# Moving SiLU, one-hot weighting and the causal mask of a transformer tower to GpSimd

## The reference, cut to what matters

```
h = tok(x)
h = h + L0_attn(layernorm(h))
h = h + L0_ffn(layernorm(h))       # routed part: silu(x w1) * (x w3), weighted, summed over tokens
h = h + L1_attn(layernorm(h))      # scores att, causal; polymax below
h = h + L1_ffn(layernorm(h))       # rms norm, ternary up, gelu, rms norm, ternary down

def polymax(x):                    # masked scores are -inf and give 0
    lin  = where((x >= -100) & (x <= 0), -0.01 * x + 1, 0)
    poly = where(x > 0, x ** 2 + 1, 0)
    return (poly + lin) / 1000
```

## Time and profile before

| | before |
|---|---|
| median of 3 runs | 842.32 us |
| the profiled execution, its own time | 843.61 us |
| its span, first to last instruction | 841.5 us |
| mean granted TensorE clock | 0.933 |
| TensorE busy in products | 735.3 us (87%) |
| VectorE busy | 647.9 us (77%) |
| ScalarE busy | 409.8 us (49%) |
| GpSimd busy | 77.9 us (9%), 68 instructions |

### The profile page before, as it was taken

One profiled execution on the slowest core, in us unless ns is written; L12 is line 12 of the kernel. 1 busy time (PEld: TensorE's weight loads), 2 busy tenths in 40 slices (PEclk: granted clock), 3 DMA queues, 4 the chain that ended last, 5 costly groups with the idle time before them and its releaser, 6 DMA issues.

```text
span 841.5 us, 24887 instructions
## 1 busy us (share of the span) xinstructions
PE 735.3 (87%) x10567; PEld 514.5 (61%) x10567; DVE 647.9 (77%) x1447; ACT 409.8 (49%) x609; POOL 77.9 (9%) x68
## 2 busy tenths in 40 slices
PE   5879999999999999975795788999998999997857
PEld 3456666667676757654384556566765756565634
DVE  7667878888878888677586778988888998587653
ACT  4536454555546473542223282845547382644513
POOL 1101111110202020100000001000101001010000
PEclk9869999999999999975875999999999999999969
DMA  9024202020202000200000000000000000000000
GB/s 323 12 95 156 76 0 75 0 75 0 75 0 75 0 0 6 97 2 1 1 2 1 2 2 26 3 26 3 0 25 0 25 2 26 2 26 2 20 9 26
DMA packets 7371, 27.22 MB, mean 32 GB/s; under 512 B 2320, under 2 KB 3216, under 8 KB 5776
## 3 DMA queue, kind: packets, MB, share of 16 engines
q1 hardware_dynamic: 7312, 26.35, 8.4%
HBM read 22.15 MB, written 4.19 MB: 31 GB/s over the span
## 4 chain that ended last, share of the span: by engine, by line
PE 60%; DVE 22%; issue 9%; ACT 8%; DMA 0%; POOL 0%; DVEq 0%; POOLq 0%; SPq 0%; ACTq 0%
PE PS L372 10%; PE PS L321 6%; PE PS L741 6%; PE PS L383 5%; PE PS L476 4%; PE PS L706 4%; PE PS L362 4%; PE PS L465 3%; PE PS L418 3%; PE PS L433 3%; DVE mx L1290 3%; DVE Pm L1296 2%; ACT w_s L1015 2%; PE PS L451 2%; PE PS L683 2%
## 5 line engine op out<-in xcount | busy, mean ns | idle before, releaser
L890 ACT ACTIVATE PT<-PS 128x512 f32<-128x512 f32 x64 | 36.8, 596 | 78.4 <-PE PS L465 78.4
L362 PE MATMUL PS<-ident_s,xn 128*128 128x128 f32 x256 | 48.2, 304 | 25.5 <-DVE xn L1211 22.3
L719 PE MATMUL PS<-xT,wqkv_h 128*128 128x512 f16 x256 | 63.7, 394 | 6.0 <-ACT w_s L1015 4.5
L321 PE MATMUL PS<-tokW_h,w_s 128*128 128x256 f16 x504 | 58.5, 273 | 0.0
L883 ACT ACTIVATE Pm<-Pm 128x1024 f32<-128x1024 f32 x32 | 33.5, 1056 | 51.3 <-DVE Pm L1296 51.3
L362 PEld LDWEIGHTS PS<-ident_s,xn 128*128 128x128 f32 x256 | 31.0, 149 | 38.1 <-DVE xn L1211 21.0
L321 PEld LDWEIGHTS PS<-tokW_h,w_s 128*128 128x128 f16 x504 | 48.7, 98 | 5.8
L741 PE MATMUL PS<-tokW_h,work 128*128 128x256 f16 x448 | 51.4, 273 | 0.5 <-issue 0.5
L1290 DVE TENSOR_REDUCE mx<-PS 128x16 f32<-128x1024 f32 x32 | 39.0, 1220 | 16.3 <-PE PS L433 16.2
L372 PE MATMUL PS<-xT,wat_h 128*128 128x512 f16 x192 | 46.2, 400 | 4.5 <-DVE xT L1592 4.5
L719 PEld LDWEIGHTS PS<-xT,wqkv_h 128*128 128x128 f16 x256 | 22.7, 100 | 44.0 <-ACT w_s L1015 17.9
(11 more groups left out here) (245 smaller groups left out, 1636.8 us busy)
## 6 DMA issues: line engine op xcount, KB each, us to landing
work<-in_x SPq DMA_DIRECT2D x7, 1536.0 KB, 6.9
out<-H SPq DMA_DIRECT2D x8, 512.0 KB, 2.6
w_s<-in_w SPq DMA_DIRECT2D x3, 1024.0 KB, 7.0
work<-in_x SPq DMA_DIRECT2D x3, 512.0 KB, 5.9
wup_s<-in_wup SPq DMA_DIRECT2D x1, 1024.0 KB, 4.8
wdn_s<-in_wdn SPq DMA_DIRECT2D x1, 1024.0 KB, 8.3
w_s<-in_tokW SPq DMA_DIRECT2D x3, 256.0 KB, 4.1
wup_s<-in_wqkv SPq DMA_DIRECT2D x1, 768.0 KB, 7.5
```

What stands on the lines that cost most here:

```text
L321: m = pe.matmul(dst, halves_[xi][:, k, rows], w[:, wi, k, cols], start=(n == 0), stop=(n == 3 * chunks - 1))
L362: m = pe.transpose(PS[:, bank, t * P:(t + 1) * P], xn[:, t, c * P:(c + 1) * P], ident_s[:, :])
L719: m = pe.matmul(PS[:, UP_BANKS[f % 3], :], wup_h[:, c, f * P:(f + 1) * P], part[:, c, :], start=(k == 0), stop=(k == 2 * C - 1))
```

## The change

1. The mask products on TensorE (`identb`, `cmaskb`) are gone, and the score products start fresh. GpSimd subtracts the mask (-1e30) from the linear part in SBUF instead, in place, one instruction of 128x1024 f32 per tile (`mask_later`, 32 in all), and `poly` waits for it (`masked`). Masked positions then hold about 1e30, and (lin <= 1) makes them 0.
2. Both linear parts of tiles 0 and 1 are taken by VectorE (`v_lin`), none of them by ScalarE. For tiles 2 and 3 ScalarE takes the linear part before the square.
3. `silus` leaves VectorE. On GpSimd it is two instructions per half, a product and a sum (`silu`), four per routed slot. `weighted_hots` goes to GpSimd too, at the end of the slot before.
4. `stats3` of a slot's input is done a slot ahead, behind `v_x4T`, and `norm3` is then the first work of a slot.
5. `norm4` has two small steps in the place of four. `poly` of tiles 0 and 1 stands behind all eight `g_parts`, not with four of them between.

```
@@ B2_scores @@
                 elif t == 2:
-                    pe.wait_ge(lin_ok, 3 * g + 1)
-                    pe.wait_ge(linv_ok, g + 1)
+                    pe.wait_ge(linv_ok, 2 * g + 2)
                 hb = (t % 2) * 256
-                for i in range(4):
-                    pe.matmul(PS[:, i, hb:hb + 256], identb[:, :], cmaskb[:, :, :], start=True, stop=False,
-                              skip_group_check=True)
...
-                                          start=False, stop=True, tile_position=(32 * i, 0), skip_group_check=True)
+                                          start=True, stop=True, tile_position=(32 * i, 0), skip_group_check=True)
@@ scalar: a_B3, slot_B @@
                         relus(g + 1, 1)
-                        lins(g + 1, 0)
...
                 for t in (2, 3):
                     relus(g, t)
+                    lins(g, t)
                     quads(g, t)
-                    lins(g, t)
@@ gpsimd @@
+            def mask_later(g, t):
+
+                if t < 2:
+                    pool.wait_ge(linv_ok, 2 * g + t + 1)
+                else:
+                    pool.wait_ge(lin_ok, 2 * g + t - 1)
+                v = lin[t % 2][:, :].rearrange("p (n q) -> p n q", q=L)
+                pool.tensor_tensor(v, v, cmask_s[:, 0, :].unsqueeze(1).broadcast_to([P, NH, L]), ALU.subtract)\
+                    .then_inc(masked, 1)
+
+            def silu(g, k):
+
+                cols = slice(k * RB * HID // 2, (k + 1) * RB * HID // 2)
+                pool.wait_ge(tz_ok, 2 * g - 1 + k)
+                pool.tensor_tensor(tz[:, cols], tz[:, cols], wz[:, cols], ALU.mult).then_inc(silu_step, 1)
+                pool.wait_ge(silu_step, 4 * g - 3 + 2 * k)
+                pool.tensor_tensor(wz[:, cols], wz[:, cols], tz[:, cols], ALU.add).then_inc(silu_step, 1)
+
+            def weighted_hots(g):
+
+                pool.wait_ge(silu_step, 4 * g - 4)
+                pool.wait_ge(oh_ok, g - 1)
+                pool.tensor_tensor(one_hot_w, one_hot, wt[:, bass.ds(RB * (g - 2), RB)].unsqueeze(2)
+                                   .broadcast_to([P, RB, 64]), ALU.mult).then_inc(weighted_ok, 1)
+
             def slot_B(g, prev, nxt, routed=None):
-                if nxt:
-                    p_rstd(ve3_ok, g + 2, ve, rstd, rstd3_ok)
+                mask_later(g, 2)
                 if prev:
                     p_rg(g - 1)
+                mask_later(g, 3)
                 p_ln4(g, 0)
                 p_ln4(g, 1)
...
+                if routed in ("first", "batch"):
+                    silu(g, 0)
+                if nxt and not (isinstance(g, int) and g == LAST - 1):
+                    p_rstd(ve3_ok, g + 3, ve, rstd, rstd3_ok)
+                if routed in ("first", "batch"):
+                    silu(g, 1)
+                if nxt:
+                    mask_later(g + 1, 0)
+                    mask_later(g + 1, 1)
+                if routed in ("first", "batch"):
+                    weighted_hots(g + 1)
@@ vector: poly, v_lin, norm4, slot_B @@
-                if t == 1:
-                    dve.wait_ge(linv_ok, g + 1)
-                else:
-                    dve.wait_ge(lin_ok, 3 * g + max(t, 1))
+                dve.wait_ge(masked, TILES * g + t + 1)
...
+                for t in range(2):
+                    hb = t * 256
+                    if not first(g):
+                        dve.wait_ge(f2_ok, TILES * g + t - 1)
+                    dve.wait_ge(relu_ok, TILES * g + 2)
+                    dve.tensor_scalar(lin[t][:, :].rearrange("p (i n) -> p i n", i=4), PS[:, 0:4, hb:hb + 256],
+                                      0.0, -0.01, ALU.min, ALU.mult).then_inc(linv_ok, 1)
...
                 v_x4T(g)
-                if routed in ("first", "batch"):
-                    silus(g)
+                if nxt and not (isinstance(g, int) and g == LAST - 1):
+                    stats3(g + 2)
                 if nxt:
                     v_quads(g + 1, 0)
                     v_quads(g + 1, 1)
                     v_lin(g + 1)
-                g_parts(g, 0, 4)
+                g_parts(g, 0, NF)
                 if nxt:
                     poly(g + 1, 0)
-                g_parts(g, 4, NF)
-                if nxt:
                     poly(g + 1, 1)
```

More of the change, by code:

```diff
@@ L84, in build @@
         wup_s = sb("wup_s", [P, C, FF]); wdn_s = sb("wdn_s", [P, NF, E])
-        ident_s = sb("ident_s", [P, P]); identb = sb("identb", [P, P], BF16); identh = sb("identh", [P, P], F16)
+        ident_s = sb("ident_s", [P, P]); identh = sb("identh", [P, P], F16)
         par_s = sb("par_s", [P, 4])
@@ L91, in build @@
         delta_s = sb("delta_s", [P, NH]); rev64_s = sb("rev64_s", [P, L])
-        cmask_s = sb("cmask_s", [P, 4, L]); cmaskb = sb("cmaskb", [P, 4, L], BF16)
+        cmask_s = sb("cmask_s", [P, 4, L])
         ridx_s = sb("ridx_s", [P, 64]); iota_s = sb("iota_s", [P, 64]); rev8_s = sb("rev8_s", [P, NX])
@@ L223, in build @@
         k_out, keep_ok, lg_ok, lin_ok, loaded_A, loaded_B = sems("k_out keep_ok lg_ok lin_ok loaded_A loaded_B")
+        masked = sem("masked")
         hs_high, linv_ok = sem("hs_high"), sem("linv_ok")
@@ L592, in routed_sums @@
             def routed_sums(g):
-                pe.wait_ge(lin_ok, 3 * g + 3)
+                pe.wait_ge(lin_ok, 2 * g + 2)
                 pe.wait_ge(weighted_ok, g - 1)
@@ L822, in _ @@
             attend_second(LAST, lambda c: transpose_chunk(0, c, xn1, FIRST_BANKS[c], xn3_ok, x3T_mm))
-            pe.wait_ge(setup_b, 4)
+            pe.wait_ge(setup_b, 2)
             pe.wait_ge(low_w, PARTS + len(splits) - 1)
@@ L1147, in _ @@
                 dve.memset(buf[:], v).then_inc(setup_v, 1)
-            for k, v in ((0, -0.5), (1, 0.5)):
+            for k, v in ((0, 0.5), (1, 0.5)):
                 dve.memset(pq[:, k, :], v).then_inc(setup_v, 1)
@@ L1549, in gates_in @@
                     dve.tensor_tensor(half_batch(k), z, weighted(k, g), ALU.mult).then_inc(wz_ok, 1)
-            def silus(g):
-                for k in range(2):
-                    cols = slice(k * RB * HID // 2, (k + 1) * RB * HID // 2)
-                    dve.wait_ge(tz_ok, 2 * g - 1 + k)
-                    dve.scalar_tensor_tensor(out=wz[:, cols], in0=tz[:, cols], scalar=1.0, in1=wz[:, cols],
-                                             op0=ALU.add, op1=ALU.mult).then_inc(silu_step, 1)
-            def weighted_hots(g):
-                dve.wait_ge(silu_step, 2 * g - 2)
-                dve.tensor_tensor(one_hot_w, one_hot, wt[:, bass.ds(RB * (g - 2), RB)].unsqueeze(2)
-                                  .broadcast_to([P, RB, 64]), ALU.mult).then_inc(weighted_ok, 1)
             def gated_sums():
@@ L1619, in v_lin @@
             def v_lin(g):
-                if not first(g):
-                    dve.wait_ge(f2_ok, TILES * g)
-                dve.wait_ge(lin_ok, 3 * g + 1)
-                dve.tensor_scalar(lin[1][:, :].rearrange("p (i n) -> p i n", i=4), PS[:, 0:4, 256:512], 0.0, -0.01,
-                                  ALU.min, ALU.mult).then_inc(linv_ok, 1)
+                for t in range(2):
[5 more added lines that the diff above has]
+                                      0.0, -0.01, ALU.min, ALU.mult).then_inc(linv_ok, 1)
             def turned(g, pair, bank):
@@ L1652, in norm4 @@
                 dve.wait_ge(rstd4_ok, 2 * g + pair + 1)
-                n = 8 * g + 4 * pair
-                dve.tensor_tensor(rr[:, ts], rq[:, 1, ts], rq[:, 0, ts], ALU.mult).then_inc(r4_step, 1)
+                n = 4 * g + 2 * pair
+                dve.scalar_tensor_tensor(out=rr[:, ts], in0=rq[:, 0, ts], scalar=1e-8, in1=rq[:, 1, ts], op0=ALU.mult,
+                                         op1=ALU.add).then_inc(r4_step, 1)
                 dve.wait_ge(r4_step, n + 1)
-                dve.tensor_scalar(rr[:, ts], rr[:, ts], 1e-8, None, ALU.add).then_inc(r4_step, 1)
+                dve.reciprocal(r4[:, ts], rr[:, ts]).then_inc(r4_step, 1)
                 dve.wait_ge(r4_step, n + 2)
-                dve.reciprocal(rr[:, ts], rr[:, ts]).then_inc(r4_step, 1)
-                dve.wait_ge(r4_step, n + 3)
-                dve.tensor_tensor(r4[:, ts], rr[:, ts], rq[:, 0, ts], ALU.mult).then_inc(r4_step, 1)
-                dve.wait_ge(r4_step, n + 4)
                 normalize(g, xn2, mv2, r4, xn4_ok, tiles)
@@ L1703, in slot_B @@
                 if nxt:
-                    stats3(g + 1)
+                    norm3(g + 1)
                 if prev:
@@ L1707, in slot_B @@
                 turned(g, 0, 4)
-                if nxt:
-                    norm3(g + 1)
-                if routed in ("batch", "last"):
-                    weighted_hots(g)
-                projected(g, 0, 5)
                 if routed == "batch":
@@ L1716, in slot_B @@
                     one_hots(g - 1)
+                projected(g, 0, 5)
                 if prev:
@@ L1792, in _ @@
             row_codes()
+            stats3(1)
             slot_B(0, False, True)
```

7 lines of the change are left out of this document (3 added, 4 removed).

## The result

| | before | after |
|---|---|---|
| median, runs of the two side by side | 843.17 us (4 runs) | 884.52 us (4 runs, 883.77 to 888.42) |
| profiled execution, its own time | 843.61 us | 885.16 us |
| its span | 841.5 us | 883.4 us |
| mean granted clock | 0.933 | 0.886 |

The ratio is 1.0513, 95% interval 1.0486 to 1.0541: **slower by 41 us**. The forecast was 866, in a range of 828 to 880. The side and the mechanism were right, the size fell short by 18.5 us.

The account below looks back on a forecast made before the run. TensorE and VectorE, both nearly full, were taken to bound the slot. 843.6 + 1.9 at the start + 4 x 5.1 + 3 x 1.0 - 1.3 = 867.6; that execution lay 1.3 above the median, so 866 us, range 828 to 880.

Parts of the forecast that it names:

- The bound and the free gain: TensorE and VectorE both nearly full in a routed slot; with GpSimd's work free the change saves 1.65 us a slot.
- Exclusive both ways: VectorE's two-input SBUF instructions and GpSimd's reads exclude each other, whichever comes first; routed slots become 5.1 us longer.
- the full wait: A two-input VectorE instruction arriving during a GpSimd product waits for its rest, up to 1.8 us; the lower bound was 0.
- Rival 1: GpSimd's products run beside VectorE without delaying it: 829.4 us, 12.9 less than the median; chance 0.25.
- rival 2: VectorE has precedence and only GpSimd's products stretch, by 9 us of two-input work: 845 us; chance 0.10.
- Rival 3: Milder forecast variant: VectorE's back-to-back low parts run through before GpSimd gets in, 855 us; inside the forecast's shared 0.65.
- I take 1.9 to 2.0, the lone one: Length in us of each new 1024-column GpSimd product, taken from an earlier product's 1.90 us alone.
- T': Start of the next slot's transposes, counted from this slot's; forecast +52.7 us in routed slots against 47.6 before.
- The two-input instructions of VectorE are just those at the end of the slot: Only two squares, eight low parts and four halves of poly in a slot can conflict with GpSimd's products.
- the two savings named for it: Before slot 0, fewer mask products (1.0 us) and the square behind the linear part (1.06) give back 1.9 of 3.8.
- 1.0 us slower each: Slots 0, 5 and 6, which prepare a next slot with masks alone, lose this through low parts waiting for masks.
- Variant 4: Harder forecast variant: TensorE's clock halves in its gap, down products 3.6 us longer in four slots: 880 us; inside the shared 0.65.

Follow-up runs that it names:

- narrow products: The changed kernel with every new GpSimd product cut to 16 of its 1024 columns, all semaphores and places kept: 826.5 us, ratio 0.9798.
- idle reads: The kernel before plus three unread GpSimd products of 1024 columns in each slot that prepares a next one: 886.7 us, ratio 1.0559.
- idle writes: The kernel before with GpSimd fills at that same place, each pair behind a 4-column product, nobody waiting: 840.1 us, ratio 0.9990.
- 832-column run: The changed kernel with every GpSimd product of 1024 columns cut to 832, 1.95 us each alone: 866.8 us, ratio 1.0289.
- The cut of that mask: The changed kernel with the mask product of tile 2, beside the normalization, cut to 16 of 1024 columns: 873.2 us, ratio 1.0401.
- the second batch: For the clock, the changed kernel with five filler TensorE products of 256 columns behind each slot's first seven grams: 882.9 us, ratio 1.0515.
- the three parts of this one that put nothing on GpSimd: The kernel before with statistics a slot ahead, linear part before square in tiles 2 and 3, norm4 two steps shorter: 831.4 us, ratio 0.9893.

## Why the prediction was wrong, and where it was right

**The bound and the free gain: right.** "This is what the change is worth with GpSimd free of charge": 1.65 us a slot and 829.4 in all. The narrow products gave 826.5 (821 to 829).

**Exclusive both ways: right, and it was the decisive step.** No row of before showed a two-input VectorE instruction arriving while GpSimd was at work; the forecast took "the full wait" over 0. The low parts of 2.84 us and the idle reads show that wait; the idle writes show that fills do not cause it. The rule of the Trainium skill (SBUF — State Buffer, Who interferes with whom), that whoever comes first has the way for the whole instruction, holds here in the second direction too. Rival 1 (829.4, no wait) and rival 2 (845, GpSimd alone gives way) fall, since both needed all low parts at 0.68 us. Rival 3 (VectorE keeps its place in a run) falls too: in a back-to-back run of low parts GpSimd gets in after each one.

**The step that failed: "I take 1.9 to 2.0, the lone one".** The product took 2.35 us alone. Its nearest row, the product in the earlier trace rows, writes bf16 from two broadcast inputs; the new ones read one or two full f32 operands and write f32. I had called 1.90 the lower bound and then taken it. Which of the differences makes the 0.45 us was not separated. The figure of the Trainium skill (GPSIMD Engine Reference, 3.1 Elementwise) led to an estimated 2.25, nearer. The run with 1.95 us products takes 866.8 us against the 866 forecast: 17.7 of the 18.5 us of error go with the length. The forecast had priced a product of 2.25 us at 6 us more; it is 17.7 for 2.35. In slot 3 at least seven VectorE instructions are held (four low parts, two four-column steps, L1239 and L1700, and the normalization), and the longer chain of products reaches one low part more: the last low part ended at +47.0 where the forecast had +45.15, and T' was +54.3 against +52.7.

**What that agreement hides.** "The two-input instructions of VectorE are just those at the end of the slot" left out poly of tiles 2 and 3, which meet no product, and the one-hots (L1560), beside which GpSimd waits (the mask of tile 3 lasts 2.88 us). What counts is another omission: the normalization reads one tensor from SBUF (and two columns of scalars) and is held just as long. The cut of that mask saved 9 to 11 us with products of full length; with 1.95 us ones the wait is still there (3.03 us in slot 3). The forecast had put this term at nothing. On the other side, the 832-column run holds just what the forecast said, the second square and three low parts, yet its slots 1 to 4 sum to 206.7 us where the forecast's 47.6 + 5.1 make 210.8: in slot 3 the poly of tile 1 ended at +49.0, not +50.0. The start, slot 0 and the stretch behind slot 5 came out 1.2, 1.3 and 1.7 us above the forecast. So the near equality of 866.8 and 866 is in part luck: 4 us too many in four slots against 4 too few elsewhere.

**By place**, the changed kernel against the forecast: the start +3.3 us (T of slot 0 at 464.1; 458.9 + 1.9 forecast), of which other runs with the same start show up to 2.5 less (and the two savings named for it, 1.0 and 1.06, make 2.06, not 1.9); slot 0 +2.3; slots 1 to 4 +5.5 together; slot 5 +2.5; from there to the end +4.2. Most of the miss lies where I had put little, outside the four routed slots: "1.0 us slower each" was 3.4 in slots 0 and 5, where two low parts wait 1.25 and 2.17 us and the normalization 2.06. In slot 5, 1.7 us of it are the products at half clock shown above.

**Variant 4, "the clock falls in the new gap": it did, in every slot, and it was not the price.** The down products took 5.0 to 6.1 us instead of 3.67. The variant had put 3.6 us on the path of each of four slots, and that did not fit the forecast's own offsets, by which the down products ended at +49.1 and the transposes waited until +52.7: just 3.6 us in hand. They ran 1.3 to 2.5 us longer, and ScalarE's last linear part ends at about the same moment. My first reading of that, in the second batch, was wrong as well (7 to 14 us expected; the medians differ by 1.7, the ratios not at all). In the kernel before with idle reads, where values and normalization follow behind the down products, the same fall does cost.

**What stays open:** what the low clock costs at the head of slot 0 and in the tail, and how much of the mask of tile 2 lies behind slot 5. Between the two profiled executions, slots 1 to 4 are 4.6 us shorter together with that mask cut, slot 0 1.3, slot 5 2.8 (1.7 of it the half-clock products, which that execution lacks) and the rest 2.2; the 2.5 before slot 0 are not the cut's, since other runs without it show them too.

## What to carry to other kernels

Before work is moved to an idle GpSimd, list what VectorE reads from SBUF at that time, one-input instructions among it, and charge each that arrives behind a GpSimd product up to the full length of that product; "GpSimd 9% busy" is no free room beside a VectorE at 77%. Price a product by a row with the same operands and output type, not by the same number of columns. And take a change apart before dropping it: the three parts of this one that put nothing on GpSimd are worth 1.1% by themselves.

## What the runs showed of the hardware

- GpSimd's products and VectorE's low parts (two inputs from SBUF) take strict turns when both have work queued: period 2.75 us, of which VectorE gets 0.4, one instruction. A low part is then 2.83 us long, with no semaphore to show for it.
- `tensor_scalar` from SBUF is held too, 128x256 f32 (0.41 to 2.47 us, L1243) and four-column ones (0.17 to 1.33, L1239; 0.16 to 0.56, L1700). Those that read PSUM alone (L1640, 1.21 us), an addition of a PSUM and an SBUF input (L1652, 0.69 us) and the statistics (L1231, from SBUF, 1.40 us for four) are not, with a product running beside them.
- GpSimd fills of 1024 bf16 and 384 f32 columns (0.95 and 0.41 us) beside low parts cost nothing.
- TensorE's granted clock fell to 0.50 in each of slots 0 to 6 of the changed kernel, where it had only grams with waits between them, for 6.8 to some 13.6 us at a time. Five filler products behind seven grams kept the down products at full clock in six of seven slots; eight behind the first four did so in slots 0, 5 and 6, and not in 1 to 4.
